# A loop over 16 steps of linear attention, run in pairs of steps

## What is computed

```python
def favor_plus(x, W):                      # W: 64 x 128 random features
    sq = 0.5 * jnp.sum(x * x, axis=-1, keepdims=True)
    return jnp.exp(x @ W - sq) / sqrt(128)
# x is 32 sequences of 32 tokens, 256 wide; ctx is 32 x 257 x 256
x = x + cross_attention(layernorm(x), ctx)              # softmax(q k^T) v, one head
h = layernorm(x)
q, k, v = heads(h @ Wq), heads(h @ Wk), heads(h @ Wv)   # 16 heads of 64
qp, kp = favor_plus(q, W_feat), favor_plus(k, W_feat)
# causal linear attention, token by token:
#   S += kp_t v_t^T;  z += kp_t;  y_t = (qp_t S) / (qp_t . z + 1e-6)
x = x + y @ Wo
x = x + bitlinear(gelu(bitlinear(layernorm(x), w1)), w2)   # ternary weights, 8-bit activations
```

## Time and profile before

| | us |
|---|---|
| median of 3 runs | 252.69 |
| lowest, highest | 252.28, 252.93 |
| the profiled execution | 252.84 |
| its span | 251.0 |
| PE busy | 240.3 |
| DVE, ACT, POOL busy | 187.2, 146.6, 101.6 |

### The profile page before, as it was taken

The page is one execution under the profiler, slowest core; times in us unless marked ns, Lnnn a source line. Parts: engine busy times, 40 slices in busy tenths (PEclk is TensorE's granted clock), DMA queues, the critical chain, the costliest instruction groups (busy, mean ns, idle before and its releaser), DMA issues.

```text
span 251.0 us, 7011 instructions
## 1 busy us (share of the span) xinstructions
PE 240.3 (96%) x2736; PEld 189.2 (75%) x2736; DVE 187.2 (75%) x474; ACT 146.6 (58%) x285; POOL 101.6 (40%) x139
## 2 busy tenths in 40 slices
PE   8998889999999999999999999999999999999985
PEld 7854557777687778777777787777788988888845
DVE  5677888666733585867888888775578999999985
ACT  0553453544445788567556666755747257787772
POOL 2073113342202558443673568727530034444430
PEclk9999999999999999999999999999999999999999
DMA  6999999991079001100110000000000000000002
GB/s 179 367 384 404 396 396 394 340 393 45 1 224 331 33 0 46 44 3 1 44 44 3 1 3 3 3 0 3 4 3 3 4 0 3 21 21 24 22 24 65
DMA packets 15521, 26.83 MB, mean 107 GB/s; under 512 B 1248, under 2 KB 8832, under 8 KB 15488
## 3 DMA queue, kind: packets, MB, share of 16 engines
q1 hardware_dynamic: 14720, 25.96, 29.1%
q10 hardware_dynamic: 768, 0.43, 0.6%
HBM read 25.33 MB, written 1.05 MB: 105 GB/s over the span
## 4 chain that ended last, share of the span: by engine, by line
PE 62%; DVE 14%; DMA 5%; SPq 5%; POOL 5%; issue 4%; ACT 4%; DVEq 0%; POOLq 0%; ACTq 0%
PE b L1364 11%; PE b L1124 8%; PE b L1126 7%; PE b L1125 7%; PE b L1408 6%; DMA wv_raw<-in_aWv 5%; PE b L1383 4%; PE b L1285 3%; PE b L1288 2%; PE b L1495 2%; PE b L1281 2%; SPq L270 2%; PE b L1536 2%; SPq L276 2%; DVE yT_lo L996 1%
## 5 line engine op out<-in xcount | busy, mean ns | idle before, releaser
L868 DVE TENSOR_TENSOR x_lo<-b,x_hi 128x512 fp32r<-128x512 f32 x32 | 21.7, 688 | 16.8 <-ACT x_hi L472 16.7
L609 ACT ACTIVATE phi<-b 128x512 f32<-128x512 f32 x48 | 26.0, 597 | 11.3 <-PE b L1364 11.3
L354 POOL TENSOR_TENSOR lnr<-lnv,mh 128x1 f32<-128x1 f32 x16 | 8.8, 551 | 55.6 <-DVE lnv L732 55.6
L412 POOL TENSOR_TENSOR sq_lo<-sq_sum,sq_hi 128x512 fp32r<-128x512 f32 x16 | 20.6, 1286 | 25.8 <-ACT sq_hi L472 25.8
L530 ACT ACTIVATE sq<-b 128x512 f32<-128x512 f32 x32 | 19.3, 603 | 18.2 <-PE b L1126 18.2
L406 POOL TENSOR_TENSOR sq_sum<-sq,sq 128x512 f32<-128x512 f32 x16 | 20.7, 1294 | 21.7 <-ACT sq L530 21.7
L1124 PE MATMUL b<-nT_lo,wp_hi 128*128 128x512 f32 x64 | 26.8, 419 | 0.1
L1126 PE MATMUL b<-nT_hi,wp_hi 128*128 128x512 f32 x64 | 25.1, 392 | 0.0
L1125 PE MATMUL b<-nT_hi,wp_lo 128*128 128x512 f32 x64 | 25.0, 391 | 0.0
L942 DVE TENSOR_TENSOR smk<-b,mask 64x512 f32<-64x512 f32 x32 | 22.0, 688 | 2.9 <-PE b L1383 1.2
L1408 PEld LDWEIGHTS b<-va,smk 128*64 128x64 f32 x512 | 17.5, 137 | 7.4 <-issue 7.0
(11 more groups left out here) (181 smaller groups left out, 617.9 us busy)
## 6 DMA issues: line engine op xcount, KB each, us to landing
cT<-in_ctxT SPq DMA_DIRECT2D x8, 1028.0 KB, 14.2
cn<-in_ctx SPq DMA_DIRECT2D x8, 1024.0 KB, 14.9
wv_raw<-in_aWv SPq DMA_DIRECT2D x1, 1024.0 KB, 13.7
wp_raw<-in_aWq SPq DMA_DIRECT2D x4, 256.0 KB, 4.7
wp_raw<-in_aWk SPq DMA_DIRECT2D x4, 256.0 KB, 4.7
w_raw<-in_w2T SPq DMA_DIRECT2D x1, 1024.0 KB, 5.6
wo<-in_aWo SPq DMA_DIRECT2D x1, 1024.0 KB, 8.1
w_raw<-in_w1T SPq DMA_DIRECT2D x1, 1024.0 KB, 5.0
```

The costliest lines, as they stand in the source:

```text
L412: nc.gpsimd.tensor_tensor(sq_lo[n % 2][:], sq_sum[:], sq_hi[n % 2][:].bitcast(F32), ALU.subtract).then_inc(sq_l, 1)
L609: nc.scalar.activation(phi(n, a)[:], feature_bank(a), ACT.Exp).then_inc(f_exp, 1)
L868: nc.vector.tensor_tensor(x_lo[n % 2][r][:], proj_bank(n, r), x_hi[n % 2][r][:].bitcast(F32), ALU.subtract).then_inc(x_l, 1)
```

## The change

Iterations 3 to 14 are taken in pairs (n, n + 1). On PE a pair is both projections, `exponents(n - 1)`, a block `group(j)` with j = (n - 3) // 2, and `exponents(n)`. The block has scores 2j, numerators 4j - 2, scores 2j + 1, and numerators 4j - 1, 4j and 4j + 1. In the first pair there are no numerators of a pair before, and the small matmul `w_bc` stands in their place. Steps 1, 2 and 15 stay single.

The banks are shared anew. Odd steps project into b0 and b1, even ones into b6 and b7. Scores alternate between b0 and b1, values between b6 and b7 (v below 22). `x_hi` and `x_lo` have three buffers instead of two, indexed n % 3, and the waits on `f_mm` before they are written look three steps back instead of two. Numerators 4j and 4j + 1 wait for the division two heads before (`n_y` of v - 1), numerators 4j - 2 and 4j - 1 for the roundings of step n + 1.

ACT and DVE follow in their lists. DVE masks scores 2j, divides heads 4j - 2 and 4j - 1, masks scores 2j + 1, and divides 4j and 4j + 1. The memory of wo is now that of w1's raw weights, so wo is loaded once w1 has been quantised (`w_quant` 4), and its high parts are all split in step 10, its low parts in steps 13 and 14. w1 and w2 change places in the loads and in `weight_sum`. POOL's list is otherwise as before.

```diff
--- before
+++ after
@@ -191,16 +195,17 @@
             return (b7, b3[:])[half][:, 0:P]
 
         def proj_bank(n, r):
-            return (b5, b7)[r] if n == 0 else (b0, b1)[r][:]
+            return (b5, b7)[r] if n == 0 else ((b6, b7)[r], (b0, b1)[r][:])[n % 2]
 
         def feature_bank(a):
             return (b2[:], b3[:], b4, b5)[a]
 
         def score_bank(u):
-            return {13: b0[:], 14: b2[:], 15: b4}.get(u, b6)
+            return {12: b6, 13: b0[:], 14: b2[:], 15: b4}.get(u, (b0, b1)[u % 2][:])
 
         def value_bank(v):
-            return {23: b1[:], 25: b6, 26: b1[:], 27: b0[:], 29: b3[:], 30: b5, 31: b6}.get(v, b7)[:, 0:HALF * VW]
+            late = {23: b1[:], 25: b6, 26: b1[:], 27: b0[:], 29: b3[:], 30: b5, 31: b6}
+            return late.get(v, b6 if v % 2 == 0 and v < 22 else b7)[:, 0:HALF * VW]
 
         def head_order(n):
             return (2, 3, 0, 1) if n < STEPS - 1 else (0, 1, 2, 3)
...
@@ -312,14 +317,15 @@
                 load_cn(g)
             load_quad(0, 1)
             sp.wait_ge(av_cp, NG)
+            sp.dma_start(w1_raw[:], w1T.rearrange("(c p) n -> p c n", p=P)).then_inc(ld_w1, 16)
+            sp.wait_ge(nT_mm, NG)
             sp.dma_start(w2_raw[:], w2T.rearrange("(c p) n -> p c n", p=P)).then_inc(ld_w2, 16)
-            sp.dma_start(wo[:], aWo.rearrange("(c p) n -> p c n", p=P)).then_inc(ld_wo, 16)
-            sp.wait_ge(nT_mm, NG)
-            sp.dma_start(w1_raw[:], w1T.rearrange("(c p) n -> p c n", p=P)).then_inc(ld_w1, 16)
             for q in range(1, QUADS):
                 for t in range(2):
                     sp.wait_ge(w_split, 8 * (q - 1) + 4 * t + 4)
                     load_quad(q, t)
+            sp.wait_ge(w_quant, 4)
+            sp.dma_start(wo[:], aWo.rearrange("(c p) n -> p c n", p=P)).then_inc(ld_wo, 16)
             outv = out.rearrange("(g p) d -> g p d", p=P)
             for g in range(LAST):
                 sp.wait_ge(fin_r, g + 1)
...
@@ -412,13 +418,17 @@
                 nc.gpsimd.tensor_tensor(sq_lo[n % 2][:], sq_sum[:], sq_hi[n % 2][:].bitcast(F32),
                                         ALU.subtract).then_inc(sq_l, 1)
 
-            def split_wo(k):
+            def split_wo_high():
+                pool.wait_ge(ld_wo, 16)
+                for k in range(4):
+                    at = slice(2 * k, 2 * k + 2)
+                    nc.gpsimd.tensor_copy(wo_hi[:, at], wo[:, at]).then_inc(wo_split, 1)
+
+            def split_wo_low(k):
+                at = slice(2 * k, 2 * k + 2)
                 if k == 0:
-                    pool.wait_ge(ld_wo, 16)
-                    pool.wait_ge(w_quant, 4)
-                at = slice(2 * k, 2 * k + 2)
-                nc.gpsimd.tensor_copy(wo_hi[:, at], wo[:, at]).then_inc(wo_split, 1)
-                pool.wait_ge(wo_split, 2 * k + 1)
+                    pool.wait_ge(w_quant, 8)
+                    pool.wait_ge(wo_split, 4)
                 nc.gpsimd.tensor_tensor(wo_lo[:, at], wo[:, at], wo_hi[:, at].bitcast(F32),
                                         ALU.subtract).then_inc(wo_split, 1)
 
...
@@ -429,8 +439,14 @@
                     split_quad(n // 4, 1)
                 squares_sum(n)
                 squares_low(n)
-                if n in (9, 10, 13, 14):
-                    split_wo((9, 10, 13, 14).index(n))
+                if n == 10:
+                    split_wo_high()
+                if n == 13:
+                    split_wo_low(0)
+                    split_wo_low(1)
+                if n == 14:
+                    split_wo_low(2)
+                    split_wo_low(3)
 
 
             def round_a(g):
...
@@ -609,12 +625,28 @@
                     nc.scalar.activation(phi(n, a)[:], feature_bank(a), ACT.Exp).then_inc(f_exp, 1)
 
             squares_high(0)
-            for n in range(1, STEPS):
+            for n in (1, 2):
                 squares(n, 0)
                 squares(n, 1)
                 features(n - 1, 0, 1)
                 squares_high(n)
                 features(n - 1, 2, 3)
+            for n in range(3, STEPS - 1, 2):
+                if n > 3:
+                    features(n - 2, 0, 1, 2, 3)
+                squares(n, 0)
+                squares(n, 1)
+                squares(n + 1, 0)
+                squares(n + 1, 1)
+                squares_high(n)
+                features(n - 1, 0, 1, 2, 3)
+                squares_high(n + 1)
+            features(STEPS - 3, 0, 1, 2, 3)
+            squares(STEPS - 1, 0)
+            squares(STEPS - 1, 1)
+            features(STEPS - 2, 0, 1)
+            squares_high(STEPS - 1)
+            features(STEPS - 2, 2, 3)
             features(STEPS - 1, 0, 1, 2, 3)
 
 
...
@@ -966,28 +998,40 @@
                     rden[:, v % 2, :].rearrange("p (g o) -> p g o", o=1).broadcast_to([P, HALF, HD]),
                     ALU.mult).then_inc(n_y, 1)
 
-            for n in range(1, STEPS):
+            for n in (1, 2):
                 low(n, 0)
-                if n == 4:
-                    weight_scales()
                 low(n, 1)
                 if n == 1:
                     dve.wait_ge(ld_mask, 16)
                     clear_scores()
+                    weight_sum(0, w1_raw[:], ld_w1)
+                else:
                     weight_sum(1, w2_raw[:], ld_w2)
-                if n == 2:
-                    weight_sum(0, w1_raw[:], ld_w1)
-                u = n - 3
-                if u >= 1:
-                    outputs(2 * u - 2)
-                if u >= 0:
-                    masked(u)
-                if n == STEPS - 1:
-                    masked(u + 1)
-                if u >= 1:
-                    outputs(2 * u - 1)
+            for n in range(3, STEPS - 1, 2):
+                j = (n - 3) // 2
+                low(n, 0)
+                low(n, 1)
                 if 5 <= n < 13:
-                    quantise_w(n - 5)
+                    quantise_w(n - 4)
+                low(n + 1, 0)
+                low(n + 1, 1)
+                masked(2 * j)
+                if j >= 1:
+                    outputs(4 * j - 2)
+                    outputs(4 * j - 1)
+                else:
+                    weight_scales()
+                masked(2 * j + 1)
+                outputs(4 * j)
+                outputs(4 * j + 1)
+                if n < 11:
+                    quantise_w(n - 3)
+            low(STEPS - 1, 0)
+            low(STEPS - 1, 1)
+            outputs(22)
+            masked(12)
+            masked(13)
+            outputs(23)
 
             def yTc(g, c):
                 if g >= 2:
...
@@ -1293,9 +1337,15 @@
                 for r in rs:
                     if r == 0 and h == 0:
                         pe.wait_ge(w_split, 8 * q + 4 * t + 4)
-                    if n >= 2:
-                        pe.wait_ge(sq_f, 2 * (n - 1) + r + 1)
-                        pe.wait_ge(x_l, 2 * (n - 1) + r + 1)
+                    if n == 2:
+                        pe.wait_ge(x_l, 2)
+                    if n >= 3:
+                        pe.wait_ge(sq_f, 2 * (n - 2) + r + 1)
+                        pe.wait_ge(x_l, 2 * (n - 2) + r + 1)
+                    if n >= 5 and n % 2 == 1:
+                        pe.wait_ge(s_mask, 2 * (n - 5 + r) + 2)
+                    if n >= 6 and n % 2 == 0:
+                        pe.wait_ge(n_y, 2 * (n - 6) + r + 1)
                     for c in range(DC):
                         mm = three(proj_bank(n, r), wp_hi[:, t, c, r, :], wp_lo[:, t, c, r, :],
                                    nT_hi[:, c, TOK * h:TOK * (h + 1)], nT_lo[:, c, TOK * h:TOK * (h + 1)],
...
@@ -1371,8 +1421,8 @@
                     pe.wait_ge(f_exp, 8 * (j + 1))
                 else:
                     pe.wait_ge(f_exp, 2 * (u - 14) + 62)
-                if u < 13:
-                    pe.wait_ge(s_mask, 2 * u)
+                if u < 12:
+                    pe.wait_ge(x_l, 4 * j + 7 + pair)
                 if u == 13:
                     pe.wait_ge(x_l, 2 * STEPS - 1)
                 for a in range(2):
...
@@ -1390,9 +1440,16 @@
                 pe.wait_ge(s_mask, 2 * u + 2)
                 if v == 0:
                     pe.wait_ge(s_zero, 4)
+                if v == 1:
                     pe.wait_ge(w_scale, 1)
-                elif v == 23:
+                if v == 23:
                     pe.wait_ge(x_l, 2 * STEPS)
+                elif v < 2 or (v < 22 and v % 4 >= 2):
+                    step = 2 * ((v + 2) // 4) + 4
+                    pe.wait_ge(sq_f, 2 * step + v % 2 + 1)
+                    pe.wait_ge(x_l, 2 * step + v % 2 + 1)
+                elif v < 22:
+                    pe.wait_ge(n_y, v - 1)
                 elif v <= 24:
                     pe.wait_ge(n_y, min(v, 23))
                 elif v == 26:
...
@@ -1410,26 +1467,38 @@
                                        start=True, stop=True)
                 mm.then_inc(n_mm, 1)
 
-            def slot(n):
-                u = n - 3
-                if u >= 1:
-                    numerators(2 * u - 2)
```

(44 more changed lines are left out.)

26 lines of the change are left out of this document (15 added, 11 removed).

## The result

The changed kernel took 256.06 us, the median of 4 runs (254.91 to 257.67), beside 252.70 for the kernel before. The ratio is 1.014, with an interval from 1.0088 to 1.0192, so the change made the kernel slower, by less than 2%. The forecast was 255.5, in a range from 253.2 to 257.6.

A forecast was written before the change was run, and what follows sets the result against it. PE's sequence bounds the loop: matmuls at their own pace plus losses between kinds. The profiled 252.84 + 2.1 (first pair) + 0.7 (five pairs) gave 255.6, as a median 255.5 us, range 253.2 to 257.6.

The forecast's parts named there:

- The total: Whole kernel: 252.84 + 2.1 for the first pair + 0.7 for five pairs, 255.6; as a median 255.5 us.
- Losses at changes of kind: PE in a complete pair: 0.20, 0.15, 0.20 and 0.23 us where one kind of matmul follows another, 0.78 in sum.
- The waits in the block: Numerators 4j and 4j + 1 wait for DVE's divisions, 0.77 and 0.28 us, starting 3.62 and 4.37 after scores 2j.
- rivals 1 and 2: Rival 1: both waits for `y` vanish, 250.0 (chance 0.10); rival 2: DVE's chain is 0.5 shorter, 253.0 (0.12).
- A pair: Each of five complete pairs takes 14.80 us, 0.13 longer than two single steps, +0.7 us in all.
- The first pair: Steps 3 and 4: PE idles 2.2 us before projection 4 for split weights; projection 5 at 106.3, +2.1 us.
- Nothing for the roundings, the loads and the quantising: Third set of rounded tiles, reordered weight loads, DVE's roundings and quantising: hidden, no cost, with 0.3 us left at worst.
- Rival 3: GpSimd's split comes late for projection 12 in the pair of step 9; 1 to 2 us lost, 257.2; chance 0.13.
- if the clock left 1.00 after the idle time: Sign against the forecast: the granted clock falling after PE's idle time; no size or chance given.
- the gain of 0.96 a pair: Fewer changes of kind on PE save 0.96 us in each pair, which would take 13.71 without a new wait.

The follow-up runs named there:

- fill8: The changed kernel with 8 identity matmuls of no use put into PE's wait before projection 4; 255.21 us, ratio 1.0099 to the kernel before.
- both: The changed kernel with exponents(2) between projections 3 and 4 and exponents(n) ahead of numerators 4j and 4j + 1; 250.60 us, ratio 0.9916 to before.
- inside: The changed kernel with exponents(n) moved into the block, ahead of numerators 4j and 4j + 1; 251.38 us, ratio 0.996 to the kernel before.

## Why the prediction came out, step by step

**The total** was 255.5 and came out at 256.06. Against the executions in which the clock held, 255.27, it is 0.2 off, against the others 1.5. That the 0.2 is so small is in part luck, since the 0.6 gained ahead of projection 3 was not in the sum and offsets what was short in it: from projection 3 to 5 it takes 15.96 with the clock held (`fill8`), 2.3 more than before and not 2.1.

**Losses at changes of kind.** Read in the rows of the changed kernel above: projection to exponents 112.88 to 113.77 is 0.89 for work of 0.69, 0.20 as forecast. Exponents to scores, 114.92 to 116.23, is 1.31 for 1.16, 0.15 as forecast. Numerators to exponents, 119.61 to 120.79 less 0.47 and 0.46, is 0.25, where 0.20 was allowed. Exponents to projection, 121.96 to 122.63, is 0.67 for 0.46, 0.21 and not 0.23. Together 0.81 for 0.78. The Trainium skill's page "TensorEngine Tiling (Array Packing)" (Key Properties) names the drain on a change of mode, and the trace agrees; it also shows that the price, here 0.15 to 0.25, depends on the pair of shapes.

**The waits in the block** were the step on which the sign hung. 3.62 and 4.37 were forecast, 3.62 and 4.36 measured. All four terms of the DVE chain kept their size although the banks had changed: masks of 0.68 to 0.71, a division in 0.41 from `den` to the start of `y`, 0.14 to 0.15 for the release. With that rivals 1 and 2 fall: DVE was not 0.5 shorter, and no wait vanished.

**A pair** is 14.75 to 14.79, forecast 14.80, +0.55 in all for +0.7. **The first pair**: by starts PE is idle for 2.36 before projection 4 (5.14 less 2.78; the view of waits shows 2.13), where 2.2 was forecast, and with the clock held (`fill8`) 10.81 from projection 4 to 5 for 10.7.

**Nothing for the roundings, the loads and the quantising** was right: within the five pairs PE waits for `y` and for nothing else.

**Rival 3** (0.13) didn't occur, but by 0.1 us and not by the 1.1 of its sum. It had GpSimd ready at 16.5, due at 17.6; counted from the pair's start (137.07) the split ended at 17.49 and projection 12 started at 17.65. The casts began at 12.5 and not at 11.9, and the split took 2.8 and not 2.1. So the price was too low by 1.0, and that the rival stayed away was luck. Where a pair is 1 us shorter, it is there, in `both` and `inside`, with 0.66 us of idle time.

**The step that was missing** is the clock. The prediction said that it would be wrong if the clock left 1.00 after the idle time, but gave that no price and no chance. It costs 1.6 to 1.7 us in half of the executions. In the profiled one its 1.6 us are most of what the first pair took beyond the forecast. The prediction held because its range was wide enough for either group. That the median of four lies 0.6 from the forecast is luck: two executions of each kind put it between the groups, 0.8 from one and 0.9 from the other. A text that had priced it would have had 255.3 and 257.0 as two cases of the same mechanism.

The prediction also sought where the gain of 0.96 a pair would be lost, but not what would bring it back. It was one line: the exponents stood behind the numerators that waited, and not ahead of them.

## What to carry to other kernels

When work is grouped by kind to save changes of kind, write down for each group the time at which the other engine's answer comes, counted from the group's start, and compare it with the work that is left for this engine: here 0.96 us a pair were saved and 1.05 came in as waiting, and moving one independent piece into the gap was worth 1 us a pair; with two repairs more, +1.4% became -1.3%. After every microsecond that is taken out, look again at the engine that had one microsecond to spare. And on a PE that is hardly ever idle, give a single wait of 2 us a second price, the one for the clock after it.
